# One loop over first-level groups: the next group's routing and dispatch between the pieces of this group's experts

## What is computed

```
xn = l2norm(layernorm(x)) * scale * gamma_in
logits1 = einsum('bGgd,esd->bGges', xg, phi)          # tokens against 8 x 16 slots
disp1, comb1 = softmax over tokens, softmax over slots
yn  = l2norm(einsum('bGgd,bGges->bGesd', xg, disp1)) * scale * gamma2
means = yn.reshape(b, G, E1, m, 4, d).mean(axis=4)
se2 = l2norm(einsum('bGkmd,kdf->bGkmf', means, w_slot2)) * scale    # routing
logits2 = einsum('bGksd,bGkemd->bGksem', yn, se2)                  # within group k only
disp2, comb2 = softmax(logits2, axis=3), softmax(logits2 over e, m)
slots2 = einsum('bGksd,bGksem->bGkemd', yn, disp2)                 # dispatch
v, gate = split(einsum(slots2, w1[k, e]) + b1)                     # experts
o = einsum(v * gelu(gate), w2[k, e]) + b2
out = x + combine(o, comb2, comb1)
```

## Time and profile before

| | us |
|---|---|
| median of three runs | 3254.47 |
| the three runs | 3253.41, 3254.47, 3260.67 |
| span of the profiled execution | 3262.2 |
| of it up to the first DMA of routing | 1904.0 |
| routing | 1904 to 2084 |
| dispatch | 2084 to 2300, first expert matmul at 2317.7 |
| experts | to 3170.8 |
| last stage | to 3262.2 |

### The profile page before, as it was taken

The page is one execution under the profiler, slowest core; times in us unless marked ns, Lnnn a source line. Parts: engine busy times, 40 slices in busy tenths (PEclk is TensorE's granted clock), DMA queues, the critical chain, the costliest instruction groups (busy, mean ns, idle before and its releaser), DMA issues. The chain is left out here.

```text
span 3262.2 us, 63713 instructions
## 1 busy us (share of the span) xinstructions
PE 2983.9 (91%) x21571; PEld 2873.5 (88%) x21571; DVE 1913.3 (59%) x3165; ACT 1531.1 (47%) x3966; POOL 1444.8 (44%) x1406
## 2 busy tenths in 40 slices
PE   3999999999999999999999847788899999999986
PEld 2899999999999999999999836688799999999982
DVE  4456556565656565565656447445577766666754
ACT  3454545545454545454454434355544544444530
POOL 0334444443434343444444347200377766666750
PEclk9999999999999999999999969889999999999999
DMA  3000101010101011010101057455566666666869
GB/s 122 28 23 31 36 24 43 24 43 24 43 24 43 23 35 32 24 43 24 43 24 39 20 209 282 137 154 164 185 209 215 210 187 186 210 194 189 260 225 365
DMA packets 293646, 358.96 MB, mean 110 GB/s; under 512 B 24328, under 2 KB 285960, under 8 KB 293512
## 3 DMA queue, kind: packets, MB, share of 16 engines
q1 hardware_dynamic: 284840, 344.92, 33.0%
q10 hardware_dynamic: 8704, 12.58, 1.0%
HBM read 286.14 MB, written 71.30 MB: 110 GB/s over the span
## 5 line engine op out<-in xcount | busy, mean ns | idle before, releaser
L1607 PE MATMUL u_bank<-x_in,x_w 128*128 128x256 f32 x4608 | 584.1, 286 | 25.1 <-issue 19.5
L1607 PEld LDWEIGHTS u_bank<-x_in,x_w 128*128 128x128 f32 x4608 | 578.5, 195 | 26.5 <-issue 26.5
L925 POOL TENSOR_TENSOR hT_lo<-h_tmp,hT_hi 128x512 fp32r<-128x512 f32 x192 | 247.8, 1290 | 483.3 <-DVE hT_hi L813 483.3
L1760 POOL TENSOR_TENSOR x_w<-raw,x_w 128x768 fp32r<-128x768 f32 x128 | 274.0, 2141 | 297.3 <-DVE x_w L1703 297.3
L1764 POOL TENSOR_TENSOR x_aT<-x_act,x_aT 128x512 fp32r<-128x512 f32 x128 | 299.5, 2339 | 212.0 <-ACT x_aT L1672 212.0
L389 PE MATMUL m_bank<-yT_hi,w_hi 128*128 128x256 f32 x1152 | 339.9, 295 | 0.0
L1663 ACT ACTIVATE x_gelu<-u_bank,x_b1T 128x256 f32<-128x256 f32 x256 | 121.9, 476 | 439.3 <-PE u_bank L1607 439.3
L389 PE MATMUL m_bank<-yT_lo,w_hi 128*128 128x256 f32 x1152 | 324.5, 282 | 0.0
L389 PE MATMUL m_bank<-yT_hi,w_lo 128*128 128x256 f32 x1152 | 323.9, 281 | 0.0
L660 ACT ACTIVATE h_tmp<-m_bank,b1c 128x256 f32<-128x256 f32 x384 | 160.9, 470 | 330.2 <-PE m_bank L389 329.8
L1619 PE MATMUL o_bank<-x_w,x_aT 128*128 128x384 f32 x1536 | 287.9, 335 | 1.8 <-POOL x_aT L1764 1.8
(11 more groups left out here) (212 smaller groups left out, 7408.8 us busy)
## 6 DMA issues: line engine op xcount, KB each, us to landing
raw<-in_L_ffn_w_dram SPq DMA_DIRECT2D x384, 384.0 KB, 5.1
ws_raw<-in_L_ffn_w_slot_dram SPq DMA_DIRECT2D x8, 2304.0 KB, 9.6
x_in<-in_x_dram SPq DMA_DIRECT2D x32, 384.0 KB, 3.4
x_res<-in_x_dram SPq DMA_DIRECT2D x32, 384.0 KB, 4.1
residual<-f_sb SPq DMA_DIRECT2D x32, 384.0 KB, 2.5
yn<-yn_sb SPq DMA_DIRECT2D x32, 384.0 KB, 2.5
yk<-yn SPq DMA_DIRECT2D x16, 768.0 KB, 11.2
se<-se SPq DMA_DIRECT2D x16, 768.0 KB, 3.3
```

The source lines that it names most:

```text
L925: nc.gpsimd.tensor_tensor(hT[i % 3][1][:], h_tmp[i % 2][:], hT[i % 3][0][:].bitcast(F32), ALU.subtract).then_inc(hl.sem, 1)
L1607: mm = pe.matmul(u_bank[n % BANKS][:, g, :], w1s[i % 2][a][:, c, g, c2 * P:(c2 + 1) * P], xT[e % 2][b][:, c, :], start=c == 0 and j == 0, ...
L1760: nc.gpsimd.tensor_tensor(w2s[i % 2][1][:], raw2[i][:], w2s[i % 2][0][:].bitcast(F32), ALU.subtract).then_inc(w2_lo.sem, 1)
```

## The change

`routes`, `dispatch` and `experts` are replaced by one function, `mixture`. Its body(k, n) does the four experts of group k and, between their pieces, routing and dispatch of the next group n = k + 1. The sequence is body(none, 0), body(0, 1), a loop of two iterations with two bodies each, body(5, 6), body(6, 7), body(7, none). Each engine's stream is written out by hand in this order.

- Dispatch works per group on eight tiles of 8 blocks x 16 slots (index j, two halves t of four tiles) rather than per block on all groups; the matmul counts of dispatch are the same. se2 no longer goes through DRAM: scaled rows `se` are transposed into `seT` in SBUF. The input rows go straight from PSUM to `x_in` of the next group (one set of buffers for each parity), and `slots2T` is gone.
- On PE the inserted operations are, in this order: T0-T7 (transposes of yn, L1331), G0-G7 (routing, nine matmuls each, L1343), S0-S7 (transposes of se, L1353), L0, L1 (logits of a half, L1364), P0, P1 (their transposes, L1375), D0, D1 (transposes of dispatch weights, L1384), C0, C1 (by comb1, L1393), O0-O7 (input rows of a tile, L1403). They share three banks `n_bank` in a fixed rotation; each waits until the last user of its bank has been read.
- `u_bank` has three buffers instead of four, `o_bank` one pair instead of two, raw w2 two buffers instead of four, w_slot2 is loaded in quarters into one buffer `ws_raw`.
- The w2 high cast moves from DVE to ACT, and POOL does its low part ahead of the activation's low part instead of behind it. Means are summed by DVE reductions from ynT. The small addition ahead of the power moves from DVE to POOL.
- The first 32 residual blocks are loaded during the last group, 20 more when the last weights have been split, 12 in `combine` instead of 8. A release of semaphores stands between layer and mixture.

```
-        with ExitStack() as ctx:
-            routes(nc, ctx, sb, ps, sem, ident, nhalf, eps, f_w_slot2, yn_dram, se_dram)
...
+        free_semaphores()
+        with ExitStack() as tail_ctx:
+            arena = sb(tail_ctx, "arena", [P, EARLY_A * D])
+            pieces_arena = sb(tail_ctx, "pieces_arena", [P, (EARLY - EARLY_A) * D])
...
+            def w2_high(x, i):
+                act.wait_ge(raw2_landed[i % 2].sem, raw2_landed[i % 2].at(x, 16 * (i // 2 + 1)))
+                if i >= 2:
+                    act.wait_ge(down_done.sem, down_done.at(x, i - 1))
...
+                if i < 2:
+                    w1_high(x, i + 2)
+                elif not is_last(x):
+                    w1_high(x + 1, i - 2)
+                if i < PIECES - 1:
+                    w2_high(x, i + 1)
...
+                nc.scalar.copy(aTs[i % 2][0][:], aT[i % 2][:]).then_inc(ah.sem, 1)
...
+                if i < PIECES - 1:
+                    w2_low(x, i + 1)
+                elif not is_last(x):
+                    w2_low(x + 1, 0)
+                pool.wait_ge(ah.sem, ah.at(x, i + 1))
+                nc.gpsimd.tensor_tensor(aTs[i % 2][1][:], aT[i % 2][:], aTs[i % 2][0][:].bitcast(F32), ALU.subtract
+                                        ).then_inc(al.sem, 1)
...
+            def body(k, n, par):
+                up(k, 0, 0, 0, par); turn(n, 0); up(k, 0, 0, 1, par); turn(n, 1); down(k, 0, -1); turn(n, 2)
...
+                up(k, 0, 3, 0, par); route(n, 0); up(k, 0, 3, 1, par); down(k, 0, 2); route(n, 1)
+                up(k, 1, 0, 0, par); route_T(n, 0); up(k, 1, 0, 1, par); route(n, 2); down(k, 1, -1)
+                route_T(n, 1); route(n, 3)
...
+                up(k, 2, 0, 0, par); route_T(n, 7); up(k, 2, 0, 1, par); logits(n, 0); down(k, 2, -1)
+                up(k, 2, 1, 0, par); logits_T(n, 0); up(k, 2, 1, 1, par); down(k, 2, 0)
+                up(k, 2, 2, 0, par); logits(n, 1); up(k, 2, 2, 1, par); down(k, 2, 1); logits_T(n, 1); disp_T(n, 0)
+                up(k, 2, 3, 0, par); back(n, 0); up(k, 2, 3, 1, par); rows(n, 0); down(k, 2, 2); rows(n, 1)
+                up(k, 3, 0, 0, par); rows(n, 2); up(k, 3, 0, 1, par); rows(n, 3); disp_T(n, 1); down(k, 3, -1); back(n, 1)
+                up(k, 3, 1, 0, par); rows(n, 4); up(k, 3, 1, 1, par); rows(n, 5); down(k, 3, 0); rows(n, 6)
+                up(k, 3, 2, 0, par); rows(n, 7); up(k, 3, 2, 1, par); down(k, 3, 1)
+                up(k, 3, 3, 0, par); up(k, 3, 3, 1, par); down(k, 3, 2)
```

More of the change, by code:

```diff
@@ new lines, in route @@
+            def route(n, g):
+                if n is None:
+                    return
+                e, i = divmod(g, HB)
+                pe.wait_ge(wl.sem, wl.at(n, e + 1))
+                pe.wait_ge(ml.sem, ml.at(n, i + 1))
+                bank = take(n, f"G{g}")
+                for c in range(DC):
+                    for j, (a, b) in enumerate(((0, 0), (0, 1), (1, 0))):
+                        mm = pe.matmul(bank[:, 0:D], mT[a][:, c, i, :], ws[e % 2][b][:, c, :],
+                                       start=c == 0 and j == 0, stop=c == DC - 1 and j == 2)
+                mm.then_inc(g_full.sem, 1)
@@ new lines, in route_T, with logits @@
+            def route_T(n, g):
+                if n is None:
+                    return
+                pe.wait_ge(se_ok.sem, se_ok.at(n, g + 1))
+                bank = take(n, f"S{g}")
+                for c in range(DC):
+                    mm = pe.transpose(bank[:, c * P:(c + 1) * P], se[g % 3][:, c * P:(c + 1) * P], ident[:])
+                mm.then_inc(s_full.sem, 1)
+            def logits(n, t):
+                if n is None:
+                    return
+                pe.wait_ge(seT_ok.sem, seT_ok.at(n, NG2 - 1 + t))
+                bank = take(n, f"L{t}")
+                for j in range(JT):
+                    for c in range(DC):
+                        b = 8 * (t * JT + j)
+                        mm = pe.matmul(bank[:, j * P:(j + 1) * P], ynT[:, c, t * JT + j, :],
+                                       seT[:, c, b:b + 8, :, :].rearrange("p b m e -> p (b m e)"),
+                                       start=c == 0, stop=c == DC - 1)
+                mm.then_inc(l_full.sem, 1)
@@ new lines, in back, with rows @@
+            def back(n, t):
+                if n is None:
+                    return
+                pe.wait_ge(cb_landed.sem, cb_landed.at(n, 16 * JT * (t + 1)))
+                bank = take(n, f"C{t}")
+                for j in range(JT):
+                    mm = pe.matmul(bank[:, j * P:(j + 1) * P], lg[:, j, 0, :], cb[:, j, :], start=True, stop=True)
+                mm.then_inc(c_full.sem, 1)
+            def rows(n, j):
+                if n is None:
+                    return
+                if j % JT == 0:
+                    pe.wait_ge(dT_ok.sem, dT_ok.at(n, j // JT + 1))
+                bank = take(n, f"O{j}")
+                for c in range(DC):
+                    mm = pe.matmul(bank[:, c * P:(c + 1) * P], yn[:, j, c * P:(c + 1) * P], dT[:, j % JT, :],
+                                   start=True, stop=True)
+                mm.then_inc(o_full.sem, 1)
@@ L1082, in _ @@
+            over_groups(pe, body)
+            down(E1, 0, -1)
         @block.scalar
         def _(act):
[L1084 to L1096 removed]
@@ new lines, in rows_out, with piece @@
+            def rows_out(k, e):
+                x = k * E2 + e
+                dve.wait_ge(down_done.sem, down_done.at(x, PIECES))
+                dve.wait_ge(b2_landed[e % 2].sem, 16 * (k * (E2 // 2) + e // 2 + 1))
+                if past(x, 1):
+                    dve.wait_ge(o_stored.sem, o_stored.at(x - 1, 32))
+                for t in range(2):
+                    nc.vector.tensor_tensor(o_sb[:, t, :], o_bank[t][:, 0:D], b2r[e % 2][:], ALU.add).then_inc(o_ok.sem, 1)
+            def piece(k, e, i):
+                if k is None:
+                    return
+                x = k * E2 + e
+                if i == 0 and past(x, 1):
+                    rows_out(k if e else k - 1, (e - 1) % E2)
+                if i < 2:
+                    w1_low(x, i + 2)
+                elif not is_last(x):
+                    w1_low(x + 1, i - 2)
```

1300 lines of the change are left out of this document (619 added, 681 removed).

## The result

The changed kernel takes **3351.55 us** (median of 4 runs, 3345.89 to 3356.96) against 3253.94 us for the kernel before on the same chip (4 runs, 3250.86 to 3260.67): a ratio of 1.0295, 95% interval 1.0265 to 1.0325. It is 98 us **slower**; the forecast was 39 us faster (3215 us, so the median is missed by 136.6 us). The profiled execution has a span of 3347.7 us.

The account below looks back on a forecast made before the run. Bounds: experts by PE, routing by an engine chain, dispatch by loads. Start 77 + 3 + 1, groups 7 x 147.2, last group 103.5, edge 7.5, last stage 96.8 make 1319.2 against 1358.2: 39 less, 3215 us, range 3148 to 3275.

Parts of the forecast that it names:

- 81 + 2.4: Ahead of the loop: group 0 routed alone 77 us, 3 for the lower clock, 1 for the semaphore release.
- 7 x 147.2 + 7.5: Seven merged groups, each 135.0 us of PE work, 3 for fp32 operations and 9.2 of waits; one loop edge 7.5.
- 103.5 - 2.4: Last group, with nothing to route: 102.3 us and 1.2 for the last down, together 103.5.
- 96.8: Last stage: 91.4 us as before, 2.4 for more residual blocks, 3 for late residual loads.
- 135.0 + 3: PE per merged group: experts 102.3, dispatch 20.2, routing 12.5 us, plus 3 for 32 plain fp32 operations.
- The waits that I named: PE's waits in a merged group: P1 3.8, O2 2.3, D1 1.1, downs 0.5 and 1.5 us.
- the sum of waits: Waits that interleaving adds on PE in a merged group: 9.2 us, called the term that decides.
- The edge itself: Loop's one backward edge: 4.9 us of break plus 2.6 in the matmuls behind it, 7.5 (0 to 15).
- my cycle of 6.3 us: Each expert piece: w2 cast, GpSimd's two subtracts and down at low-end durations take 6.3 us, just under PE's 6.39.
- The rival of the GpSimd recurrence: Every piece, above all the last group's 16: GpSimd's recurrence becomes the bound; at 8.5 us a piece, 3298 us; chance 0.12.
- ACT costs more around the exponentials: Merged groups: further ScalarE waits of 7 us a group give 3264 us, chance 0.08; with drain 3271, chance 0.03.
- drain: At ScalarE's table loads: another 1380 ns beyond the 1283 ns load, by the skill page; 3271 us, chance 0.03.

Follow-up runs that it names:

- e12: Changed kernel with masked logits, stores, loads, slot-weight and last-expert steps reordered, plus routing's third-tile root between GpSimd's subtracts and a slot-weight subtract behind the scale: 3236.13 us, ratio 0.9948.
- e2: Changed kernel with both halves' masked logits moved ahead on VectorE, and the first dispatch transpose and its use one up later on TensorE: 3300.06 us, ratio 1.0149.
- e3: Changed kernel with the combine store issued ahead of the next weights on SyncE, and the last group's early residual loads spread between pieces: 3330.16 us, ratio 1.0253.
- e11: Kernel before with only the w2 cast on ScalarE ahead of the activation's cast, and GpSimd's w2 subtract ahead of the activation's: 3276.24 us, ratio 1.0099.
- e1: Changed kernel with the old order inside each piece: activation cast and subtract ahead of the next w2 piece on ScalarE and GpSimd: 3358.78 us, ratio 1.034.
- e6: Changed kernel with the fourth slot-weight block one step later, and the first expert's weights loaded after the second slot-weight block: 3353.05 us, ratio 1.0338.
- e4: Changed kernel with both softmaxes' exponentials replaced by a copy, so most table loads go and the output is another: 3306.17 us, ratio 1.0173.
- e5: Changed kernel with the edits of e2 and e4 together, the output being another: 3284.46 us, ratio 1.0120.

## Why the prediction was wrong

The span was forecast at 3222.7 us (3215 and the 7.7 that lie between span and median) and came out at 3347.7: 125 us. The median is off by another 11.6, since those 7.7 us belonged to one execution and not to the kernel: here the profiled span is 3.9 us below the median. Part by part, from routing's start at 1904:

| part | forecast | measured |
|---|---|---|
| 1904 to the first transpose of group 1, 1993.97 | 81 + 2.4 | 90.0 |
| seven merged groups with one edge, to 3126.9 | 7 x 147.2 + 7.5 = 1037.9 | 1132.9 |
| last group, from the same point | 103.5 - 2.4 | 123.3 |
| last stage | 96.8 | 97.5 |

**Right in size.** PE's work in a merged group, 135.0 + 3 = 138: e12, where PE hardly idles, has 138.71. The waits that I named: P1 3.8, O2 2.3, D1 1.1, downs 2.0 came out at 3.1, 2.4, 0.8 and 2.6, 8.9 us against 9.2. Each stands where I had it; that the sum is so near is partly luck, for the first is 0.7 too high and the last 0.6 too low. GpSimd's activation subtract (median 1.29 us), table loads of 1.28 us without a gap, and the last stage.

**The step that failed** is the sum of waits, and in it two sentences: that I followed expert 2 from its chunk (1,1) on, and that between each G and its S "I find no wait there". A walk that begins in the middle takes every engine to be on time there. It began behind P0 (2.9 us), whose logits stood on VectorE behind result rows and a w1 subtract; it didn't reach O4 (1.6) and O6 (2.1, behind a store on SyncE); and for S2 and S7 (3.0 and 0.9) I counted PE's operations between G and S, not GpSimd's and VectorE's. With 0.4 for one G that is **10.9 us** in the group shown. Over the seven groups with their edge PE stood idle for 137.0 us, where 7 x 9.2 + 4.9 = 69.3 were forecast: 67.7 us too little. e2 took P0 (and most of P1), e3 O6 and e12 a part of S2 at their places, and the time followed; O4's waits are still there in e12 (7.9 us of 8.5). The second failed term is PE's clock: behind some of the waits the matmuls are slower (141.0 us of busy time in the group shown, 138.7 for the same matmuls in e12). I had counted that for the start and the loop's edge and not for the waits. Over the seven groups PE was busy for 995.9 us, where 7 x 138 + 2.6 = 968.6 were forecast: 27.3 us. Both together are the 95.0 us. The edge itself was forecast about right: a break of 4.42 us and some 2.3 in the 36 ups behind it, against 7.5.

**The part costed at next to nothing** (1.5 us in a merged group, none in the last). ScalarE's w2 cast and GpSimd's turned order: my cycle of 6.3 us, "just under" PE's 6.39, is 6.56 and 6.96 in e11, with waits of 0.3 to 0.4 us for the activation in every second piece; a cycle put together from the lowest durations had nothing to spare. In the last group of the changed kernel there is more: in the first piece of an expert VectorE's result rows push its w1 subtract onto GpSimd's w2 subtract. The one starts at 3188.77 and the other at 3188.80, and GpSimd's takes 3.42 us, where the earlier trace rows have 1.80 at the least. All this costs 10 us in the last group, and e1 gives them back. The rival of the GpSimd recurrence was right in kind, wrong in size and place: its "waits in every piece" don't occur, and in merged groups e1 takes them away without any gain.

**The last group** lost another 10 to 12 us to the residual loads. I had priced only the part behind the last weights and not the 32 blocks (6.3 MB) ahead of them, though they stand on the queue that feeds each piece.

**The start** took 6.6 us more. PE waited 11.9 us for the second slot weights, where I had allowed 3 for the weights ahead of them. e6 loads these later, and the start is 6.3 us shorter, so this term accounts for the miss.

**ScalarE's loads.** The rival "ACT costs more around the exponentials" has no drain to stand on: gelu's load starts at 2744.20, the gelu at 2745.50. But loads of 7.7 us a group cost some 6 in time as the order was written (e4), and at most 2.2 once the logits stood ahead (e5). I had seen them only in the waits P1, O2 and D1.

The start (6.6), the merged groups (95.0), the last group (22.2) and the last stage (0.7) make up the 125 us. What stays open is how much of the 11 us that PE still waits in each group of e12 could be taken without new waits; that wasn't tried.

## What to carry to other kernels

When work is laid between the steps of a loop that one engine bounds, walk **every** inserted step on **every** engine and queue through a whole period, back to where it began; a walk of the worst stretch alone got each of its own waits right to 0.7 us and missed more than half of all. Put at the head of each engine's list what another engine's result hangs on, and the bulk work (splits, result rows, large loads) behind it: that order alone moved this kernel from 3.0% slower to 0.5% faster. And price an edit in the order in which it will stand: what looked like 45 us of table loads was 16 us at the most once the chain around them was short.

## What the runs showed of the hardware

A wait on PE can cost more than itself: the 18 up matmuls behind one of 3.08 us took 3.69 us, others 2.31 to 2.41, so that it cost 4.4 us; the granted clock was 0.66 there. It doesn't have to: behind a wait of 2.90 us in the same expert the clock was 1.00 and the 18 took 2.41. Behind the stall of 8.40 us the twelve down matmuls took 3.62 us instead of 2.32, at a clock of 0.64 (3222 to 3226 us).

Where a VectorE subtract and a GpSimd subtract meet in these rows, the one that starts second is held up, whichever engine it is on, and the first keeps its pace. VectorE's w1 subtract of 2731.20 took 3.31 us, 1.76 alone, behind a GpSimd one that had begun 0.13 us earlier and took its usual time. The GpSimd one of 3188.80 took 3.42 us behind a w1 subtract that had begun 0.03 us earlier:

```profile
2731.07 1.83 POOL L1745 TENSOR_TENSOR x_w<-pieces_arena,x_w 128x768 fp32r<-128x768 f32 x1 [6.71 <-ACT x_w L1445]
```
```profile
3188.77 1.75 DVE L1578 TENSOR_TENSOR x_w<-pieces_arena,x_w 128x1536 fp32r<-128x1536 f32 x1
3188.80 3.42 POOL L1745 TENSOR_TENSOR x_w<-pieces_arena,x_w 128x768 fp32r<-128x768 f32 x1 [3.47 <-ACT x_w L1445]
```

This agrees with the Trainium skill, "SBUF — State Buffer", section "Who interferes with whom", by which a VectorE instruction with two SBUF inputs and a GpSimd one that reads SBUF exclude each other.

The breaks at the loop's edge are no property of the loop alone. The kernel before has four of 4.0 to 5.7 us; e11, whose PE program is the same, has none. Its page counts 39 packets on the queue of instruction transfers, that of the kernel before 75; these counts are of the whole program and don't say for which engine they were. Why the breaks come in one and not in the other, no run here shows.
